# Layer norm slabs of the FFN branch put among those of the attention branch, and a BF16 scratch tensor, in a fused recurrent layer

## The chip, the cores and the metric

The kernel runs on the 8 cores of one Trainium2 chip (two dies of four cores), each with a batch row and a quarter of its query tokens. There is no exchange between cores. The metric is the device time of the slowest core in microseconds, for one launch. Less is better.

## The reference

B = 2, S = 4096, E = 2048, 16 heads of 128, hidden size I = 8192. For all tokens:

```
xn = (x - mean) / sqrt(var + 1e-5)
q, k, v = xn @ W.T + b                 (heads of 128)
s = softmax(causal(q k.T / sqrt(128)) - slope * |i - j|) v @ Wo.T + bo
f = fwht(xn * SU_ug) / 64
h = silu(f @ W_gate.T * sc_g) * (f @ W_up.T * sc_u)
g = silu(fwht(h * SU_dp) / 64 @ W_down.T * sc_d)
out = x + s * g
```

fwht is the normalised Walsh-Hadamard transform.

## The kernel before, in words

Everything is held transposed, features on partitions, tokens along the row. A core needs K and V of all 4096 tokens of its batch row but the rest only for its own 1024 tokens, so it normalises 32 **attention slabs** of 128 tokens (xT, numbers 0 to 31) and 8 **FFN slabs** (xfT, numbers 32 to 39, called FFN slabs 32 to 39). The stages, one after another: (1) normalisation with K and V; (2) Q for its own tokens; (3) attention head by head; (4) the Wo product, stored to the scratch tensor s_scr in HBM; (5) the Hadamard transform of the FFN input; (6) up and gate products; (7) the second transform; (8) the down product with the final combination s * g + x.

Each engine runs its own list of operations in the order in which `OP` recorded them, and waits on the semaphores that an operation names. So the order of calls in the program is the order on every engine.

Stage 1 is built of three functions.

`ln_head(slab)` is the **head**: an x load (L383) on the GpSimd queue (POOL), 512 KB as it lies in SBUF, cast from F32 to BF16, into one of two buffers xTb; it waits until the slab before last has been normalised (ev_xnt). VectorE squares it (sq_scr, L389). TensorE sums x and squares over the features with a column of ones, 16 + 16 matmuls with 1 output row (L395, L400: the statistics). The **row chain** follows: ScalarE copies two rows out of PSUM (L408, L409), VectorE forms the variance (L415, L416), ScalarE the root (L420), VectorE rstd_row and mrstd_row (L424, L425). The rows have one buffer each.

`ln_tail(slab)` is the **tail**: TensorE broadcasts both rows to 128 partitions (L434, L436, F32 matmuls), ScalarE copies them to rstdB and mrstdB, VectorE normalises in 32 chained operations of 128x128 (L448 multiply, L452 subtract), here called the **sweep**. It writes xnT2 (two buffers) for an attention slab, or the slab's place in xnTf, which is kept for stages 2 and 5.

`emit_kv(slab, tail_for)` records the **K and V part**: 16 heads of 16 K matmuls (L469, 128x128), each evicted by ScalarE to kstg, one store of 512 KB to k_scr (L496); then 4 V groups of 16 matmuls (L508, 128x512) in two PSUM banks, each evicted by VectorE to vstg (L521, two buffers) and stored to v_scr from ScalarE's queue (L532). A V group waits until the eviction two groups before it. After the second K head the tail of another slab is recorded.

The loop over slabs is, for i from 0 to 39: head of i; for i = 0 its tail; else K and V of slab i-1 with the tail of i inside, as long as i-1 is an attention slab; from i = 33 on only head and tail. After it the load of Wq (L554), on the GpSimd queue, into the place of Wk, waits for the last V matmul; the Q matmuls (L568) wait for it.

```
    for i in range(NSLAB):
        ln_head(i)
        if i == 0:
            ln_tail(0)
            continue
        kvslab = i - 1
        if kvslab < NSLAB_A:
            emit_kv(kvslab, tail_for=i)
        else:
            ln_tail(i)
```

Stage 4: ScalarE evicts 64 tiles of 128x256 to sstg (L771, F32) and stores them to s_scr (L776). Stage 8: Wd comes in 128 loads of 512 KB into a ring of five (wdring, L980, GpSimd queue); for each of 32 output tiles of 128x512 ScalarE makes g_st (L1014) and issues the loads of ss_st from s_scr (L1021) and of xf_st (L1027); VectorE multiplies g_st by ss_st into o_st (L1033) and adds xf_st (L1037); SyncE stores.

Of the kernel before, what the change touches and what calls it, by code (L numbers as in the profile page):

```python
# [6 lines left out]
F32 = mybir.dt.float32  # L7
# [125 lines left out]
def build_program(cfg):  # L133
# [47 lines left out]
    s_dram = nc.dram_tensor("s_scr", [E, TOKF], F32, kind="Internal").ap()  # L181
# [39 lines left out]
    sstg = [cst(f"sstg{i}", [128, QG], F32) for i in range(2)]  # L221
# [6 lines left out]
    e_stage = 2 * IT * CS * 4 + 2 * FH * 2 + 8 * FH * 4  # L228
# [133 lines left out]
    ev_ld = {}  # L362
    ev_sq = {}
# [11 lines left out]
    def ln_head(slab):  # L375
# [3 lines left out]
        par = slab % 2  # L379
        psem = "xt%d" % par  # L380

# [4 lines left out]
            waits=[ev_xnt.get(slab - 2),  # L386
                   ev_bvB if slab <= 1 else None], dma=psem)
# [3 lines left out]
            waits=[ev_ld[slab], ev_sqmm.get(slab - 1)])  # L391

        def p1_stats(eng, par=par, ev_s=ev_sq[slab]):
# [5 lines left out]
            for ft in range(FT):  # L399
# [5 lines left out]
                           waits=[ev_ld[slab], ev_rows.get(slab - 1)])  # L405

        def p1_rows(eng):
            eng.activation(m_row[:], pb[0][0:1, 0:128], AF.Copy, scale=1.0 / E)  # L408
            return eng.activation(sq_row[:], pb[0][0:1, 128:256], AF.Copy,  # L409
                                  scale=1.0 / E)  # L410
# [17 lines left out]
    def ln_tail(slab):  # L428
# [30 lines left out]
        if slab >= NSLAB_A:  # L459
            ev_cons_all[slab] = ev_sqmm[slab]  # L460
# [681 lines left out]
```

How the kernel before makes its waits and increments, by code:

```python
    def chain(self, eng_name, E, ins):  # L103
        s = self.sem(self.esem[eng_name] + "ch")
        self.cnt[self.esem[eng_name] + "ch"] += 1
        v = self.cnt[self.esem[eng_name] + "ch"]
        ins.then_inc(self.sems[self.esem[eng_name] + "ch"], 1)
        E.wait_ge(self.sems[self.esem[eng_name] + "ch"], v)
# [7 lines left out]
            def body(E, lst=lst):  # L116
                done = {}
                for fn, ws, ev in lst:
                    need = {}
                    for (s, v, _b) in ws:
                        if v > need.get(s, 0):
                            need[s] = v
                    for s, v in need.items():
                        if v > done.get(s, 0):
                            E.wait_ge(self.sems[s], v)
                            done[s] = v
                    ins = fn(E)
                    if ev is not None:
                        ins.then_inc(self.sems[ev[0]], ev[2])
# [263 lines left out]
        def p1_stats(eng, par=par, ev_s=ev_sq[slab]):  # L393
            for ft in range(FT):
                eng.matmul(pb[0][0:1, 0:128], ones128_b[:],
                           xTb[par][:, ft * 128:ft * 128 + 128],
                           start=(ft == 0), stop=(ft == FT - 1))
            eng.wait_ge(sch.sems[ev_s[0]], ev_s[1])
            for ft in range(FT):
                ins = eng.matmul(pb[0][0:1, 128:256], ones128_b[:],
                                 sq_scr[:, ft * 128:ft * 128 + 128],
                                 start=(ft == 0), stop=(ft == FT - 1))
            return ins
```

## Time and profile before

| what | value |
|---|---|
| median of 2 runs | 4624.85 us (4624.21 to 4625.48) |
| the profiled execution | 4626.15 us, span of its slowest core (core 0) 4624.6 us |
| spans of the 8 cores | 4586.8 to 4624.6 us, mean granted TensorE clock 0.864 to 0.868 |
| busy share on core 0 | TensorE 74%, VectorE 40%, ScalarE 21% |
| chain that ended last, by engine | TensorE 64%, VectorE 20%, DMA 6% |

All rows are of core 0. The chain that ended last is followed back from the last instruction, at each step to what released it. In a timeline each row gives the start and the time in us, the engine, the line, the tiles and, in brackets, how long the engine had been idle and who ended that. "PE" is TensorE, "DVE" VectorE, "ACT" ScalarE, "POOL" GpSimd. The granted clock is a share of 2.4 GHz, its lower level 1.2 GHz.

### The profile page before, as it was taken

The numbers are of one execution on the slowest core, as the hardware profiler recorded it, in microseconds if no ns is written. First come the engines' busy times: TensorE is split into PE (matmuls) and PEld (weight loads), VectorE is DVE, ScalarE is ACT, GpSimd is POOL, SyncE is SP. The second block draws the span as 40 slices with busy tenths as digits, with TensorE's granted clock in tenths as the row PEclk, the third lists the DMA queues.
The fourth block names the chain that finished last, engine by engine and source line by source line (L and its number), as shares of the span: only waits on it lengthen the run. The fifth ranks groups of instructions, "written<-read, shape, count | busy, mean of one in ns | idle before, by whom it ended". The sixth has DMA issues, their size and how long they took to land.

```text
span 4624.6 us, 61688 instructions; the slowest of 8 cores (4586.8 to 4624.6 us)
## 1 busy us (share of the span) xinstructions
PE 3428.8 (74%) x22715; PEld 1790.9 (39%) x22715; DVE 1865.3 (40%) x3576; ACT 957.6 (21%) x2347; POOL 294.1 (6%) x309
## 2 busy tenths in 40 slices
PE   0499899999935677888884929999999800725887
PEld 0366666766722222222221804444444300302333
DVE  0244444444452166667773060000000089994001
ACT  0121221211201234444442211111111500000000
POOL 0000000000000000000000001111111100101111
PEclk9999999999957877877776959999999955867999
DMA  9333223232224221111104218888888500736999
GB/s 146 29 47 51 43 43 55 43 53 45 44 31 78 61 55 37 37 37 37 37 19 74 75 13 76 77 77 76 76 78 76 57 0 0 107 48 116 177 174 157
DMA packets 633738, 296.32 MB, mean 64 GB/s; under 512 B 520675, under 2 KB 610787, under 8 KB 631267
## 3 DMA queue, kind: packets, MB, share of 16 engines
q0 software_dynamic: 422880, 191.55, 36.7%
q10 hardware_dynamic: 102912, 58.74, 4.9%
q1 hardware_dynamic: 107652, 42.10, 4.3%
q8 instruction: 187, 3.06, 0.3%
q14 instruction: 107, 0.88, 0.1%
HBM read 433.54 MB, written 50.33 MB: 105 GB/s over the span
## 4 chain that ended last, share of the span: by engine, by line
PE 64%; DVE 20%; DMA 6%; issue 3%; SPq 3%; another core or an unknown queue 2%; ACT 2%; DVEq 0%; ACTq 0%; POOLq 0%
PE pb L856 19%; PE pb L469 9%; PE pb L508 8%; PE pb L695 5%; PE pb L678 5%; PE pb L992 5%; PE pb L674 4%; DMA wdring<-wdT 3%; DVE C L940 3%; DVE C L942 3%; SPq L307 3%; PE pb L568 2%; PE pb L760 2%; DVE rinv L611 2%
## 5 line engine op out<-in xcount | busy, mean ns | idle before, releaser
L856 PE MATMUL pb<-xnTf,wring 128*128 128x512 bf16 x4096 | 886.2, 380 | 1.1 <-ACT xnTf L826 1.1
L992 PE MATMUL pb<-U,wdring 128*128 128x512 bf16 x2048 | 464.1, 389 | 429.9 <-DVE U L952 247.4
L707 DVE SCALAR_TENSOR_TENSOR pb<-mwin_s,slopes_l,pb 128x256 f32<-128x256 f16 x1019 | 484.8, 482 | 434.2 <-PE pb L695 415.5
L856 PEld LDWEIGHTS pb<-xnTf,wring 128*128 128x128 bf16 x4096 | 401.2, 98 | 486.2 <-issue 4.3
L717 ACT ACTIVATE ET<-pb 128x256 bf16<-128x256 f32 x1019 | 390.2, 384 | 485.5 <-DVE pb L707 394.2
L469 PE MATMUL pb<-xnT,wk_b 128*128 128x128 bf16 x8192 | 487.1, 222 | 0.0
L469 PEld LDWEIGHTS pb<-xnT,wk_b 128*128 128x128 bf16 x8192 | 473.0, 100 | 11.2 <-issue 1.1
L992 PEld LDWEIGHTS pb<-U,wdring 128*128 128x128 bf16 x2048 | 202.1, 100 | 691.6 <-issue 468.6
L508 PE MATMUL pb<-wv_b,xnT 128*128 128x512 bf16 x2048 | 447.2, 379 | 0.0
L880 DVE TENSOR_TENSOR U<-A_st,B_st 128x1024 bf16<-128x1024 f32 x64 | 78.4, 1226 | 823.0 <-ACT B_st L872 823.0
L674 PE MATMUL pb<-ET,vh 128*128 128x256 bf16 x1019 | 331.5, 325 | 9.3 <-DMA vh<-v_scr 3.6
L695 PE MATMUL pb<-q_sb,kh 128*128 128x256 bf16 x1019 | 307.1, 323 | 25.6 <-DMA kh<-k_scr 25.6
L678 PE MATMUL pb<-ET,ones_b 128*1 128x256 bf16 x1019 | 311.2, 305 | 0.0
L508 PEld LDWEIGHTS pb<-wv_b,xnT 128*128 128x128 bf16 x2048 | 199.0, 98 | 234.2
L521 DVE TENSOR_TENSOR vstg<-pb,bvB 128x512 bf16<-128x512 f32 x128 | 88.0, 691 | 382.3 <-PE pb L508 245.3
L484 ACT ACTIVATE kstg<-pb,bk_l 128x128 bf16<-128x128 f32 x512 | 188.2, 367 | 242.4 <-PE pb L469 242.4
L448 DVE TENSOR_TENSOR xn_scr<-xTb,rstdB 128x128 f32<-128x128 bf16 x640 | 187.0, 292 | 126.5 <-ACT mrstdB L443 63.0
L1014 ACT ACTIVATE g_st<-pb,dnvec 128x512 bf16<-128x512 f32 x32 | 22.0, 687 | 881.4 <-PE pb L992 560.0
L678 PEld LDWEIGHTS pb<-ET,ones_b 128*1 128x1 bf16 x1019 | 80.5, 79 | 268.0 <-issue 247.7
L618 PE MATMUL pb<-rinv,ones_f 1*128 1x256 f32 x128 | 63.7, 590 | 161.5 <-DVE rinv L611 161.5
L1033 DVE TENSOR_TENSOR o_st<-g_st,ss_st 128x512 f32<-128x512 bf16 x32 | 22.1, 692 | 372.2 <-DMA xf_st<-xfT 201.8
L452 DVE TENSOR_TENSOR xnT<-xn_scr,mrstdB 128x128 bf16<-128x128 f32 x512 | 149.6, 292 | 53.6 <-DVE xn_scr L448 1.0
(85 smaller groups left out, 2530.9 us busy)
## 6 DMA issues: line engine op xcount, KB each, us to landing
wdring<-wdT POOLq DMA_DIRECT2D x128, 512.0 KB, 12.9
wring<-wupT POOLq DMA_DIRECT2D x64, 512.0 KB, 7.8
wring<-wgT POOLq DMA_DIRECT2D x64, 512.0 KB, 7.8
xTb<-xT POOLq DMA_DIRECT2D x32, 512.0 KB, 11.0
k_scr<-kstg ACTq DMA_DIRECT2D x32, 512.0 KB, 5.2
v_scr<-vstg ACTq DMA_DIRECT2D x128, 128.0 KB, 2.1
kh<-k_scr SPq DMA_DIRECT2D x16, 1024.0 KB, 6.5
vh<-v_scr SPq DMA_DIRECT2D x16, 1024.0 KB, 10.6
```

The source lines that it names most:

```text
L448: sch.chain("vector", eng, eng.tensor_mul(xn_scr[:], xTb[par][:, ft * 128:ft * 128 + 128], rstdB[:]))
L452: ins = eng.tensor_sub(dst, xn_scr[:], mrstdB[:])
L469: ins = eng.matmul(bank[:, 0:128], wk_b[:, (ft * H + hch) * 128:(ft * H + hch) * 128 + 128], xnT2[par][:, ft * 128:ft * 128 + 128], start= ...
L484: return eng.activation(kstg[par][:, hch * 128:hch * 128 + 128], bank[:, 0:128], AF.Identity, bias=bk_l[:, hch:hch + 1])
L508: ins = eng.matmul(bank[:, 0:512], xnT2[par][:, ft * 128:ft * 128 + 128], wv_b[:, ft * E + vch * 512:ft * E + vch * 512 + 512], start=(ft ...
L674: eng.matmul(pvb[:, 0:QG], vh[hp][:, rho * 128:rho * 128 + 128], ETs[e4][:], start=(idx == 0), stop=(idx == W - 1))
L678: return eng.matmul(pb[6 + par][0:1, 0:QG], ones128_b[:], ETs[e4][:], start=(idx == 0), stop=(idx == W - 1))
L695: return eng.matmul(pb[b4][:, 0:QG], kh[hp][:, rho * 128:rho * 128 + 128], q_ap, start=True, stop=True)
L707: eng.scalar_tensor_tensor(pb[b4][:, 0:QG], mwin_s[:, coff:coff + QG], slopes_l[:, h:h + 1], pb[b4][:, 0:QG], ALU.mult, ALU.add)),
L717: eng.activation(ETs[e4][:], pb[b4][:, 0:QG], AF.Exp)),
L856: ins = eng.matmul(pb[bk0 + u][:, 0:UCH], wring[slot][:, ft * 128:ft * 128 + 128], xnTf[:, ft * TOKF + u * UCH:ft * TOKF + u * UCH + UCH], ...
L992: ins = eng.matmul(pb[bk0 + e4][:, 0:FHT], wdring[slot][:, iti * 512 + e4 * 128: iti * 512 + e4 * 128 + 128], Uap(it, tk0, FHT), start=(it ...
```

## The change

Stage 1: `ln_head` and `ln_tail` take a second argument, the position `li` in a list `emit_order`; the buffers xTb and xnT2 and the waits on the slab before and before last now go by positions. The rows and rstdB/mrstdB have two halves. The list has two FFN slabs after each eight attention slabs: 0 to 7, 32, 33, 8 to 15, 34, 35, 16 to 23, 36, 37, 24 to 31, 38, 39. `pump(limit)` records heads up to a position and, before the head at position p, any tail at p-2 or earlier. Before K and V of slab ki all heads up to two positions after it are recorded. `emit_kv` calls `tail_cb` after its second K head, which records the waiting tails that are FFN slabs or attention slabs up to ki+1, the first of them first. The first two Q matmul groups wait for the last K evictions.

The scratch tensor s_scr, its staging sstg and the tile ss_st become BF16 instead of F32; the tiles after it move up in SBUF.

```
-    s_dram = nc.dram_tensor("s_scr", [E, TOKF], F32, kind="Internal").ap()
+    s_dram = nc.dram_tensor("s_scr", [E, TOKF], BF16, kind="Internal").ap()
...
-    rstdB = cst("rstdB", [128, 128], F32)
+    rstdB = cst("rstdB", [128, 256], F32)
...
-    sstg = [cst(f"sstg{i}", [128, QG], F32) for i in range(2)]
+    sstg = [cst(f"sstg{i}", [128, QG], BF16) for i in range(2)]
...
-    ss_st = at("ss_st", [128, 2 * FH], F32, p4c + FH * 4)
+    ss_st = at("ss_st", [128, 2 * FH], BF16, p4c + FH * 4)
...
-            waits=[ev_xnt.get(slab - 2),
-                   ev_bvB if slab <= 1 else None], dma=psem)
+            waits=[ev_xnt.get(pprev),
+                   ev_bvB if li <= 1 else None], dma=psem)
...
-            if hch == 1 and tail_for is not None:
-                ln_tail(tail_for)
+            if hch == 1:
+                tail_cb()
...
+    step = NSLAB_A // max(1, NSLAB_F // 2)
+    fi = NSLAB_A
+    for a in range(NSLAB_A):
+        emit_order.append(a)
+        if (a + 1) % step == 0 and fi < NSLAB:
+            emit_order.append(fi)
+            emit_order.append(fi + 1)
+            fi += 2
...
+    def pump(limit):
+        while li[0] < NSLAB and li[0] <= limit:
+            while tailq and tailq[0][1] <= li[0] - 2:
+                pop_tail()
+            s = emit_order[li[0]]
+            ln_head(s, li[0])
+            tailq.append((s, li[0]))
+            li[0] += 1
+
+    pump(1)
+    pop_tail()
+    for ki in range(NSLAB_A):
+        pump(min(NSLAB - 1, pos_attn[ki] + 2))
+
+        def tail_cb(ki=ki):
+            while tailq and (tailq[0][0] >= NSLAB_A
+                             or tailq[0][0] <= ki + 1):
+                pop_tail()
+        emit_kv(ki, pos_attn[ki] % 2, tail_cb)
```

TensorE's list from the V matmuls of slab 7 to K of slab 8, before (the L395/L400 pair is the statistics of a head, L434/L436 the broadcast of a tail, xTb_105 and xTb_106 the two x buffers, xnT_107 and xnT_108 the two normalised ones):

```order
L508 MATMUL pb<-wv_b,xnT_108 128x512 x64
L395 MATMUL pb<-xTb_106,ones_b 1x128 x16
L400 MATMUL pb<-sq_scr,ones_b 1x128 x16
L469 MATMUL pb<-xnT_107,wk_b 128x128 x32
L434 MATMUL pb<-rstd_row,ones_f 128x128
L436 MATMUL pb<-mrstd_row,ones_f 128x128
L469 MATMUL pb<-xnT_107,wk_b 128x128 x224
```

and in the changed kernel, where the same operations are at L400/L405, L449/L451, L491 (K) and L530 (V):

```order
L530 MATMUL pb<-wv_b,xnT_108 128x512 x64
L400 MATMUL pb<-xTb_105,ones_b 1x128 x16
L405 MATMUL pb<-sq_scr,ones_b 1x128 x16
L400 MATMUL pb<-xTb_106,ones_b 1x128 x16
L405 MATMUL pb<-sq_scr,ones_b 1x128 x16
L449 MATMUL pb<-rstd_row,ones_f 128x128
L451 MATMUL pb<-mrstd_row,ones_f 128x128
L400 MATMUL pb<-xTb_105,ones_b 1x128 x16
L405 MATMUL pb<-sq_scr,ones_b 1x128 x16
L491 MATMUL pb<-xnT_107,wk_b 128x128 x32
L449 MATMUL pb<-rstd_row,ones_f 128x128
L451 MATMUL pb<-mrstd_row,ones_f 128x128
```

One head stood before K of slab 8; now three heads and a tail do: heads of slabs 8, 9 and 10, and between the last two the tail of slab 8 itself. The same stands before K of slabs 16 and 24.

TensorE's list at the start, from the first head to the first K matmuls, before:

```order
L395 MATMUL pb<-xTb_105,ones_b 1x128 x16
L400 MATMUL pb<-sq_scr,ones_b 1x128 x16
L434 MATMUL pb<-rstd_row,ones_f 128x128
L436 MATMUL pb<-mrstd_row,ones_f 128x128
L395 MATMUL pb<-xTb_106,ones_b 1x128 x16
L400 MATMUL pb<-sq_scr,ones_b 1x128 x16
L469 MATMUL pb<-xnT_107,wk_b 128x128 x32
```

and in the changed kernel:

```order
L400 MATMUL pb<-xTb_105,ones_b 1x128 x16
L405 MATMUL pb<-sq_scr,ones_b 1x128 x16
L400 MATMUL pb<-xTb_106,ones_b 1x128 x16
L405 MATMUL pb<-sq_scr,ones_b 1x128 x16
L449 MATMUL pb<-rstd_row,ones_f 128x128
L451 MATMUL pb<-mrstd_row,ones_f 128x128
L400 MATMUL pb<-xTb_105,ones_b 1x128 x16
L405 MATMUL pb<-sq_scr,ones_b 1x128 x16
L491 MATMUL pb<-xnT_107,wk_b 128x128 x32
```

Two heads and a tail stood before K of slab 0; now three heads do, with the tail of slab 0 behind the second.

TensorE's list from the head before K of slab 6 to its V matmuls, before:

```order
L395 MATMUL pb<-xTb_106,ones_b 1x128 x16
L400 MATMUL pb<-sq_scr,ones_b 1x128 x16
L469 MATMUL pb<-xnT_107,wk_b 128x128 x32
L434 MATMUL pb<-rstd_row,ones_f 128x128
L436 MATMUL pb<-mrstd_row,ones_f 128x128
L469 MATMUL pb<-xnT_107,wk_b 128x128 x224
```

and in the changed kernel:

```order
L400 MATMUL pb<-xTb_105,ones_b 1x128 x16
L405 MATMUL pb<-sq_scr,ones_b 1x128 x16
L491 MATMUL pb<-xnT_107,wk_b 128x128 x32
L449 MATMUL pb<-rstd_row,ones_f 128x128
L451 MATMUL pb<-mrstd_row,ones_f 128x128
L449 MATMUL pb<-rstd_row,ones_f 128x128
L451 MATMUL pb<-mrstd_row,ones_f 128x128
L491 MATMUL pb<-xnT_107,wk_b 128x128 x224
```

K of slab 6 now carries two tails, that of slab 7 and that of FFN slab 32, and on VectorE their two sweeps stand one behind the other, both ahead of the four V evictions of slab 6. The same holds for slabs 14, 22 and 30. Behind the V matmuls of slab 31 nothing is left on TensorE before Q. On the GpSimd queue the Wq load still follows the last x load.

## Rows read from the trace of the kernel before

**Rows 1.** Chain that ended last, merged: start us, us, what.

```profile
1269.46 13.83 PE pb L508 x64
1304.95 1.88 PE pb L400 x16
1325.85 1.88 PE pb L400 x16
...
1446.94 112.63 PE pb L568 x512
```

**Rows 2.** Windows: us, busy (count) of PE, PEld, DVE, ACT, POOL, PEclk, DMA, GB/s.

```profile
1283.00:1390.00 107.00, 25.19 (x208) 21.23 (x207) 63.13 (x187) 5.83 (x25) 6.27 (x6) 0.53 0.21 21
```

**Rows 3.** DMA issues by line (last column: us to landing), and the GpSimd queue's timeline.

```profile
wk_b<-wkT POOLq DMA_DIRECT2D x1, 8192.0 KB, 60.9
...
wo_b<-woT POOLq DMA_DIRECT2D x1, 8192.0 KB, 53.3
...
1389.44 1.15 POOL L554 DMA_DIRECT2D wq_b<-wqT  x1
```

**Rows 4.** Waits of TensorE, 200 to 1280 us: total us, times, longest.

```profile
PE pb L434 <- DVE mrstd_row L425: 38.6, 30, 1.4
```

**Rows 5.** Timeline of one attention slab, 874 to 908 us.

```profile
873.95 1.05 PE L395 MATMUL pb<-xTb,ones_b 128*1 128x128 bf16 x16
...
874.80 1.22 DVE L389 TENSOR_TENSOR sq_scr<-xTb 128x2048 bf16<-128x2048 bf16 x1
...
876.16 1.05 PE L400 MATMUL pb<-sq_scr,ones_b 128*1 128x128 bf16 x16 [1.16 <-DVE sq_scr L389]
...
877.15 1.96 PE L469 MATMUL pb<-xnT,wk_b 128*128 128x128 bf16 x32
...
880.05 0.28 DVE L425 TENSOR_TENSOR mrstd_row<-m_row,rstd_row 1x128 f32<-1x128 f32 x1
...
881.09 12.78 PE L469 MATMUL pb<-xnT,wk_b 128*128 128x128 bf16 x224
...
881.78 0.29 DVE L448 TENSOR_TENSOR xn_scr<-xTb,rstdB 128x128 f32<-128x128 bf16 x1 [1.45 <-ACT mrstdB L443]
...
893.70 13.98 PE L508 MATMUL pb<-wv_b,xnT 128*128 128x512 bf16 x64
...
894.12 0.29 DVE L452 TENSOR_TENSOR xnT<-xn_scr,mrstdB 128x128 bf16<-128x128 f32 x1
...
895.31 1.14 POOL L383 DMA_DIRECT2D xTb<-xT  x1 [32.94 <-DVE xnT L452]
...
905.10 0.69 DVE L521 TENSOR_TENSOR vstg<-pb,bvB 128x512 bf16<-128x512 f32 x1 [3.46 <-DMA v_scr<-vstg]
```

**Rows 6.** Landing of the x loads (L383, all 40), and in 1340 to 1385 us.

```profile
DMA to landing us min/median/max: 6.8/10.5/14.4
...
xTb<-xfT POOLq DMA_DIRECT2D x2, 512.0 KB, 7.1
```

**Rows 7.** Timeline of the start, 170 to 200 us.

```profile
170.62 0.28 DVE L425 TENSOR_TENSOR mrstd_row<-m_row,rstd_row 1x128 f32<-1x128 f32 x1
...
187.19 1.86 PE L400 MATMUL pb<-sq_scr,ones_b 128*1 128x128 bf16 x16 [13.16 <-DVE sq_scr L389]
...
188.99 3.09 PE L469 MATMUL pb<-xnT,wk_b 128*128 128x128 bf16 x32
...
193.03 7.14 PE L469 MATMUL pb<-xnT,wk_b 128*128 128x128 bf16 x123
```

**Rows 8.** Waits, 4200 to 4624 us.

```profile
PE pb L992 <- DMA wdring<-wdT: 47.2, 23, 5.5
```

**Rows 9.** DMA queues, 4320 to 4600 us: packets, MB, share of 16 engines.

```profile
q10 hardware_dynamic: 4608, 8.39, 12.9%
```

**Rows 10.** Chain that ended last, in the Wo stage.

```profile
2581.43 3.80 DMA s_scr<-sstg
```

**Rows 11.** Groups of instructions by form: second transform's first step on VectorE.

```profile
L920 DVE TENSOR_TENSOR C<-U,U 128x512 f32<-128x512 bf16 x64 | 44.0, 688 | 64.8 <-ACT U L902 61.5
```

More of the change, by code:

```diff
@@ L362, in build_program @@
     ev_ld = {}
+    ev_bcE = {}
     ev_sq = {}
@@ L373, in build_program, with ln_head @@
     ev_vevac = {}
-    def ln_head(slab):
+    emit_order = []
+    def ln_head(slab, li):
         is_ffn = slab >= NSLAB_A
@@ L404, in ln_head, with p1_rows @@
         ev_sqmm[slab] = OP("tensor", p1_stats,
[L405 to L409, printed above, removed]
+                           waits=[ev_ld[slab], ev_rows.get(prev)])
+        pr = lambda t, q=par: t[0:1, q * 128:q * 128 + 128]
+        def p1_rows(eng, par=par):
+            eng.activation(pr(m_row), pb[0][0:1, 0:128], AF.Copy,
+                           scale=1.0 / E)
+            return eng.activation(pr(sq_row), pb[0][0:1, 128:256], AF.Copy,
@@ L418, in ln_head @@
         ev_var = OP("vector", p1_var, waits=[ev_rows[slab]])
-        ev_sd = OP("scalar", (lambda eng: eng.activation(
-            msq_row[:], var_row[:], AF.Sqrt)), waits=[ev_var])
-        def p1_rstd(eng):
-            sch.chain("vector", eng, eng.reciprocal(rstd_row[:], msq_row[:]))
-            return eng.tensor_mul(mrstd_row[:], m_row[:], rstd_row[:])
-        ev_rstd[slab] = OP("vector", p1_rstd, waits=[ev_sd])
-    def ln_tail(slab):
+        ev_sd = OP("scalar", (lambda eng, par=par: eng.activation(
+            pr(msq_row), pr(var_row), AF.Sqrt)), waits=[ev_var])
@@ L429, in ln_tail, with p1_rstd, p1_bc @@
+        def p1_rstd(eng, par=par):
+            sch.chain("vector", eng,
+                      eng.reciprocal(pr(rstd_row), pr(msq_row)))
+            return eng.tensor_mul(pr(mrstd_row), pr(m_row), pr(rstd_row))
+        ev_rstd[slab] = OP("vector", p1_rstd,
+                           waits=[ev_sd, ev_bcE.get(pprev)])
+    def ln_tail(slab, li):
         is_ffn = slab >= NSLAB_A
         cc0 = (slab - NSLAB_A) * 128 if is_ffn else slab * 128
-        par = slab % 2
-        def p1_bc(eng):
-            eng.matmul(pb[1][:, 0:128], ones1_f[:], rstd_row[:], start=True,
+        par = li % 2
+        prev = emit_order[li - 1] if li >= 1 else None
+        pprev = emit_order[li - 2] if li >= 2 else None
+        pr = lambda t, q=par: t[0:1, q * 128:q * 128 + 128]
+        def p1_bc(eng, par=par):
+            eng.matmul(pb[1][:, 0:128], ones1_f[:], pr(rstd_row), start=True,
@@ L435, in p1_bc @@
                        stop=True)
[L436 removed]
+            return eng.matmul(pb[1][:, 128:256], ones1_f[:], pr(mrstd_row),
                               start=True, stop=True)
         ev_bc = OP("tensor", p1_bc,
[L439 to L444 removed]
+                   waits=[ev_rstd[slab], ev_bcast_ev.get(prev), ev_ones])
@@ L446, in p1_xnt, with p1_bcev @@
+        ev_bcE[slab] = ev_bc
+        def p1_bcev(eng, par=par):
+            eng.copy(rstdB[:, par * 128:par * 128 + 128], pb[1][:, 0:128])
+            return eng.copy(mrstdB[:, par * 128:par * 128 + 128],
+                            pb[1][:, 128:256])
+        ev_bcast_ev[slab] = OP("scalar", p1_bcev,
+                               waits=[ev_bc, ev_xnt.get(pprev)])
         def p1_xnt(eng, par=par, is_ffn=is_ffn, cc0=cc0):
```

98 lines of the change are left out of this document (52 added, 46 removed).

## The prediction

> **What bounds the kernel now.** I read the page's chain shares and its slices first: TensorE carries most of the chain, but the kernel is a row of stages with different limits, so I went to the stage that the diff touches, 153 to 1447 us, and read its chain of waits. Up to 1283.3 us (1269.46 + 13.83) the K and V matmuls of 32 attention slabs follow one another. Then the statistics of the FFN slabs stand 20.9 us apart (1304.95, 1325.85) and the Q matmuls start only at 1446.9 [rows 1]. The view by windows says what that is: in 1283 to 1390 us TensorE works 25 of 107 us at a granted clock of 0.53 and VectorE 63 us: a serial chain of VectorE and tiny matmuls [rows 2]. Last comes Wq: its load is issued at 1389.44, behind the last x load on the GpSimd queue, and Q, which waits for it, starts 57.5 us after that, so it takes 57.4 [rows 1, 3]. So behind the last V matmul lie 163.6 us (1446.94 - 1283.3), of which the load is 57.4.
>
> Inside the attention part a slab takes 33.7 us, almost all of it K and V matmuls; the one wait that the change touches is that of the broadcast matmul (L434) for mrstd_row: 38.6 us over 30 slabs, 1.3 us each [rows 4].
>
> **Clocks of one slab**, counted from the end of the V matmuls before it (874.0) [rows 5]: squares end at 2.1, the second statistics start at 2.2, 32 K matmuls run 3.2 to 5.1, mrstd_row is done at 6.4 (3.1 us after the statistics end), the other 224 K matmuls start at 7.1. The sweep of 32 normalising operations runs 7.8 to 20.4, that is 12.7 us, the next x load is issued at 21.3, 0.9 us after it, and V ends at 33.7. I use these for every step below.
>
> **1. The end of the stage.** The FFN slabs 38 and 39 now normalise while slabs 30 and 31 are in K and V, and no x load stands behind the last V matmul. Wq still cannot start earlier, since it overwrites Wk. So the gap becomes 0.5 (queue) + 57.4 + 0.1 = 58.0 us instead of 163.6: **-105.6 us**. What is late next is the Wq load itself, bare. The loads of Wo and Wk, of the same size, took 53.3 and 60.9 us [rows 3], so the term lies between -109.7 and -102.1.
>
> **2. The wait for mrstd_row.** The tail that now stands after two K groups belongs to a slab whose head stood one slab earlier, so its row is long ready. That holds for slabs 0 to 5, 8 to 13, 16 to 21 and 24 to 29; in the other eight the FFN tail still follows its own head directly. Slab 0 is counted in step 5, so 23 x 1.3 = **-29.9 us**.
> What hid the x load before is gone, however. Head s+2 now stands before K of slab s, and its load can only be issued when the sweep of slab s has freed the buffer. The sweep starts at 6.7 instead of 7.8 (rstd of the new head at 6.4, then the broadcast), ends at 19.3, and the load goes out at 20.2. The statistics need it at 32.4, and a delay up to 0.8 us more is covered by the squares, which wait for the last V eviction anyway. So a landing of up to 13.0 us is free. The rows give 10.5 in the median and 14.4 at most [rows 6]; at 14.4 the slab gets back to its old length. From none late to all late this is 0 to +29.9; I take the side of the median, **+2**.
>
> **3. Slabs 6, 14, 22, 30: two sweeps in one slab.** VectorE now does slab 7 and then FFN slab 32: 6.7 + 12.7 + 12.7 = 32.1. The V evictions stand behind both. TensorE fills two banks (V from 20.1), then waits for the first eviction, 32.8 instead of 23.5; two more V groups of 3.5 us follow, and V ends at 39.8, 6.1 late. The third eviction can wait for the first store, as the one at 905.10 does for 3.46 us [rows 5]; here the matmuls before it hide most of that, and I add 0.7 of between 0 and 3.5: 6.8 each. 4 x 6.8 = **+27** (24 to 38).
>
> **4. Slabs 8, 16, 24: a drain.** Here three heads stand before K. Head 12 (position in the new list) needs the buffer of attention slab 8, which is swept only now. From the end of V: mrstd 6.4; squares of head 11 7.7; its statistics and row chain 4.3, 12.0; the sweep of slab 8 24.7; the queue 25.6; the load, alone on the DMA engines as in the FFN stretch, 7.1 [rows 6], 32.7; squares 33.9; statistics at the low clock, 35.9. K starts there instead of at 3.2, and its first 32 matmuls take 3.09 instead of 1.96, as they did after the idle time at the start [rows 5, 7]: 33.8 us each. Nothing covers it, since the only work ready on TensorE stands behind the statistics in its queue. 3 x 33.8 = **+101.5** (to 112 at the 10.5 us landing). This step gives back what step 1 brings.
> The Trainium skill ("DMA: Bandwidth & Descriptors", Anatomy of one DMA) fits such a load as about 2.0 us plus its bytes over 436 GB/s, an estimate of 3.2 us for 512 KB; the quietest rows here say 7.1, so this case's trace does not agree. By the rule the drains and the start would be some 18 us cheaper together; I go by the trace.
>
> **5. The start.** Head 1 and head 2 now stand before K of slab 0, and load 2 waits for the sweep of slab 0. mrstd of slab 0 170.9, squares 172.2, statistics 174.2, row chain 177.3, sweep 190.0, issue 190.9. The landing lies between 7.1 and 10.5 [rows 6]; I take 9, as no K or V store runs yet but all cores load together: 199.9. Squares, statistics, 32 cold K matmuls and the broadcast: 207.3, against 193.03 now [rows 7]. **+14.3** (12.4 to 15.8).
>
> **6. s_scr in BF16.** Stores in the Wo stage halve; the chain runs through one of them, for 3.8 us [rows 10], so the gain is 0 to 3.8, and I take 0.5, as a single wait of 64 stores shows. The loads of ss_st halve in the down projection, where TensorE waits 47.2 us in all for wdring and the ScalarE queue takes 12.9% of the DMA time of 280 us, half of it ss_st by bytes [rows 8, 9]. Half of ss_st is 9 us there, 13 over the 398 us of the stretch; between none of it and all of it I take **-7**, as TensorE waits only in bursts. Both together **-7.5** (0 to -17).
> The Trainium skill ("VectorE: DVE Perf Modes", Rules for kernel authors) promises tensor_tensor twice the rate on dense BF16, and the product in the combination now reads two BF16 tiles. It writes F32, though: a row with just these types took 688 ns for 512 columns [rows 11], no faster than today's product, so this trace gives nothing; by the rule the last four products would save about 1.2 us.
>
> **Sum.** -105.6 - 29.9 + 2 + 27 + 101.5 + 14.3 - 7.5 = +1.8 us. The profiled execution took 4626.15 us (span 4624.6), 1.3 above the median of the runs. So 4628.0 profiled, 4627 as a median.
>
> **Rivals.**
> A. The drains do not happen or are mostly hidden, so that the FFN work is really folded away: the sum without step 4 is -99.7, 4525 us. For it speaks only that this is how 5 of 6 boundaries work; against it the two x buffers and the order of TensorE's queue.
> B. The x load becomes the limit in every slab. It decides above a landing of 14.4 us: the slab is then 20.2 + landing - 0.8 long. At 17 us that is 36.4 against 33.7, 28 boundaries, +74, and the -27.9 of step 2 are gone: 1.8 + 27.9 + 74 = +104, 4729 us. For it: the K and V stores share the DMA engines with the load at just that time, in all eight cores. Against it: no landing of 40 above 14.4, and the same transfers meet at the same points as before.
> C. Start, double sweeps, drains, late loads and the Wq load are all at their upper bounds and s_scr brings nothing: 15.8 + 0 + 38 + 112 - 102.1 = +64, 4688 us. It is still inside 2%.
>
> **Chances.** The forecast with its bounds, and C with it: 0.88 (C with what lies near it 0.12). A 0.04, B 0.08. So faster by over 2% (under 4532) 0.04, within 2% 0.88, slower by over 2% (over 4717) 0.08; 2% is about what a measurement of this kernel can tell from no change. With all terms at their better bounds the sum is 12.4 - 29.9 + 24 + 101.5 - 109.7 - 17 = -19, 4606 us; I go 17 us (half of one drain) further towards A, to 4589. Upwards I go to C: 4688.
>
> **What would show it.** Right: Q starts 58 us after the last V matmul, at about 1456 us; three holes of some 34 us in front of K of slabs 8, 16 and 24, ended by an x load and its squares; the wait of the broadcast matmul falls from some 30 cases to some 8; slabs 6, 14, 22 and 30 are 6 to 7 us longer; K of slab 0 is in full swing at 207. Wrong: TensorE waiting for xTb at most boundaries (B), no holes (A), a wait for wdring that is still 47 us, or any change in the attention and up/gate stages, which the change does not touch.

## The result, and the profile after

The changed kernel takes 4602.16 us (median of 29 runs), the kernel before 4626.24 us (26 runs). The ratio is 0.994, with a 95% interval of 0.9921 to 0.9959: some 28 us faster, between 19 and 37. This is inside 2% and inside the stated range, but the forecast was +2 us, and the interval excludes that. Some runs of most kernels are disturbed on one die and several per cent longer; the ratios and intervals leave them out (the medians don't), and where a profile below is of such a run (the squares moved, the third buffer), only cores 0 to 3, on the other die, are read.

First the page of the changed kernel: its span and TensorE's share.

```profile
span 4590.7 us, 61740 instructions; the slowest of 8 cores (4568.0 to 4590.7 us)
...
PE 3420.6 (75%) x22715; PEld 1781.7 (39%) x22715; DVE 1864.2 (41%) x3576; ACT 956.3 (21%) x2347; POOL 294.1 (6%) x309
```

Core 0 is the slowest core in both profiles, and its span fell by 33.9 us (4624.6 to 4590.7). Stage 1 as a whole, read by where Q starts, gave 15.0 of that (1446.94 to 1431.94); all the rest, 18.9, comes behind Q. In the mean over the 8 cores the span fell by 25.3 us, 9.0 of it up to Q and 16.3 behind it.

**The end of the stage.** The chain that ended last, merged, as in [rows 1]: start us, us, what.

```profile
1351.95 12.71 PE pb L491 x224
1364.66 13.81 PE pb L530 x64
1378.48 53.22 another core or an unknown queue
...
1431.94 112.80 PE pb L621 x512
```

The last V matmul and Q are now 53.5 us apart instead of 163.6. The 53.22 us piece is the Wq load, which the chain doesn't name; the waits of TensorE do. Here they are for 150 to 1500 us (total us, times, longest), to be read beside [rows 4]:

```profile
PE pb L400 <- DMA xTb<-xT: 100.2, 5, 23.0
PE pb L621 <- DMA wq_b<-wqT: 53.5, 1, 53.5
PE pb L405 <- DVE sq_scr L394: 47.4, 35, 3.0
PE pb L530 <- DVE vstg L543: 17.2, 4, 4.4
PE pb L449 <- DVE mrstd_row L436: 8.8, 8, 1.4
```

The wait of the broadcast matmul (L449, L434 before) has gone from 30 cases to 8. In its place stand four new waits for an x load (at the start and in the three drains; the fifth case of the first line, for the very first slab, is in the kernel before too) and four for a V eviction (fourth line).

**A drain**, before K of slab 8: timeline (start us, us, engine, line, tiles; in brackets the idle time and who ended it).

```profile
467.17 1.05 PE L400 MATMUL pb<-xTb,ones_b 128*1 128x128 bf16 x16
...
474.84 1.87 PE L405 MATMUL pb<-sq_scr,ones_b 128*1 128x128 bf16 x16 [2.68 <-DVE sq_scr L394]
...
492.83 1.14 POOL L388 DMA_DIRECT2D xTb<-xT  x1 [36.82 <-DVE xnT L471]
...
500.24 1.86 PE L400 MATMUL pb<-xTb,ones_b 128*1 128x128 bf16 x16 [22.39 <-DMA xTb<-xT]
...
503.75 2.27 PE L491 MATMUL pb<-xnT,wk_b 128*128 128x128 bf16 x32
```

V of slab 7 ends at 467.2. The third head's load can go out only at 492.83, when the sweep of slab 8 has freed its buffer, and TensorE stands idle for it for 22.39 us. K starts at 503.75, 36.6 us after V.

**A slab with two sweeps**, slab 6:

```profile
397.81 0.45 PE L449 MATMUL pb<-rstd_row,ones_f 1*128 1x128 f32 x2 [0.84 <-DVE mrstd_row L436]
...
398.42 14.31 PE L491 MATMUL pb<-xnT,wk_b 128*128 128x128 bf16 x224
...
422.95 1.28 DVE L543 TENSOR_TENSOR vstg<-pb,bvB 128x512 bf16<-128x512 f32 x2
...
423.78 9.80 PE L530 MATMUL pb<-wv_b,xnT 128*128 128x512 bf16 x32 [4.14 <-DVE vstg L543]
...
433.51 1.05 PE L400 MATMUL pb<-xTb,ones_b 128*1 128x128 bf16 x16
```

The second half of the V matmuls waits 4.14 us for VectorE, which evicts only behind both sweeps. Note also that the 224 K matmuls take 14.31 us here.

**A plain slab**, slab 11, to be laid beside [rows 5]:

```profile
599.83 1.05 PE L405 MATMUL pb<-sq_scr,ones_b 128*1 128x128 bf16 x16 [1.16 <-DVE sq_scr L394]
...
600.82 1.96 PE L491 MATMUL pb<-xnT,wk_b 128*128 128x128 bf16 x32
...
602.71 0.48 PE L449 MATMUL pb<-rstd_row,ones_f 1*128 1x128 f32 x2
...
603.35 12.78 PE L491 MATMUL pb<-xnT,wk_b 128*128 128x128 bf16 x224
...
629.87 1.05 PE L400 MATMUL pb<-xTb,ones_b 128*1 128x128 bf16 x16
```

The broadcast matmul has no bracket any more: it follows the 32 K matmuls at once.

**All slabs at once.** A single slab hides what follows, so I took the start of each slab's K part from the timeline of core 0 (a period is the time from one K start to the next), and the time from its first to its last K matmul. These are worked out from the timeline, us:

| | before | changed |
|---|---|---|
| first K matmul of slab 0 | 188.99 | 199.95 |
| K start to K start, plain slabs (23 of them changed) | 33.7 in the clean ones | 32.3 (742.8 for 23) |
| slabs 6, 14, 22, 30 | 33.7 to 35.2 | 42.3, 42.7, 41.1, 42.7 (168.9) |
| slabs 7, 15, 23 (with the drain behind them) | 33.7 or 33.8 | 67.0, 67.0, 69.2 (203.2) |
| all 31 periods | 1063.6, that is 31 x 33.7 and 18.9 more | 1148.0 |
| K part: 15.3 to 15.9 | none | 24 slabs |
| K part: 16.7 to 17.0 | 26 slabs | 3 slabs (7, 15, 31) |
| K part: 18.2 to 18.4 | 6 slabs (core 4: 9) | 5 slabs (6, 14, 22, 23, 30) |
| last K start to Q | 194.4 | 84.0 |

The 18.9 us are what I had missed. The kernel before doesn't run 33.7 us per slab: six periods are 1.5 longer because the K part is (9.4 us together), and five more lie between 34.2 and 37.0 (9.3 together). The first kind is on every core: 6 to 9 long K parts, 9.4 to 13.9 us. The second is not: it makes 9.5 us on core 0 and 6.0 on core 1, and at most 0.7 on each of the other six. In the mean over the cores the kernel before is 14.7 us over 31 x 33.7. For the K parts the view by windows of the kernel before has the reason (columns as in [rows 2]); these are slab 12, with a long K part, and slab 13, with a short one:

```profile
606.80:621.20 14.40, 14.40 (x226) 14.20 (x226) 9.35 (x32) 5.49 (x16) 0.70 (x1) 0.88 0.00 1
642.00:656.00 14.00, 14.00 (x232) 13.12 (x231) 9.36 (x32) 5.86 (x17) 0.12 (x1) 1.00 0.01 3
```

TensorE is busy throughout both, and in the first its granted clock is 0.88 instead of 1.00: for a part of the K matmuls it was at the 1.2 GHz level. Ahead of it lie two waits of 1.16 and 1.37 us with 3 us of matmuls between them; but slab 13 has the same two (1.16 and 1.44 us) and keeps 1.00. The Trainium skill ("TensorE: Matmul & The Clock Gate", Part 1) calls the low level the default that activity releases, and ties its return to idleness; in this trace it returns with no more idle time than that, and not each time. In the changed kernel the plain slab is clean, and the slab with two sweeps isn't:

```profile
398.40:412.70 14.30, 14.30 (x226) 14.25 (x226) 10.48 (x36) 5.49 (x16) 1.14 (x1) 0.88 0.02 3
...
603.00:616.00 13.00, 13.00 (x229) 12.80 (x228) 9.67 (x33) 5.48 (x16) 0.00 (x0) 1.00 0.01 1
```

The longest of the other periods (slab 9, 37.0) shows in the timeline of the kernel before as a V store that landed late, with the evictions, the squares and TensorE behind it; slabs 10 and 4, the next longest, have the same with waits of 7.3 and 5.4 us (the last row, the sums of squares, takes 1.86 us instead of the 1.05 of [rows 5]: the clock is low here as well):

```profile
528.39 1.29 DVE L521 TENSOR_TENSOR vstg<-pb,bvB 128x512 bf16<-128x512 f32 x2 [8.10 <-DMA v_scr<-vstg]
...
530.95 1.86 PE L400 MATMUL pb<-sq_scr,ones_b 128*1 128x128 bf16 x16 [3.65 <-DVE sq_scr L389]
```

In the changed kernel no eviction on core 0 waits longer than 3.9 us for a V store. On the other cores the longest wait is 4.3 to 7.8 us before and 3.4 to 4.8 after.

**The rest of the kernel.** Mean over the 8 cores, us: from Q to the first down matmul 2511.0 before, 2508.4 after; first to last down matmul 631.7 and 620.2; behind it 22.5 and 20.3. Core 0, the slowest, gained more in the down product: 646.2 to 629.0. In both profiles the cores fall into four with a long down product (633.6 to 646.2 before, 626.3 to 629.0 after) and four with a short one (621.9 to 625.6, and 610.4 to 615.4). They aren't the same four: cores 4 and 7 are among the short ones before and the long ones after. Core 0's waits for Wd, against [rows 8], and the queue q10 (it carries the loads of ss_st and xf_st) at 4320 to 4560 us, in the changed kernel and then in the kernel before:

```profile
PE pb L1048 <- DMA wdring<-wdT: 33.0, 20, 3.5
...
q10 hardware_dynamic: 4608, 6.29, 10.8%
...
q10 hardware_dynamic: 4320, 7.87, 14.1%
```

### The profile page after: what moved, and what is told of

The parts are those of the page before. It is cut to its first block, busy times and chain, and to the rows that moved or that the text cites. A ratio compares the mean times of both kernels' runs of the same rounds, so it can differ in the third digit from the quotient of the medians.

```text
span 4590.7 us, 61740 instructions; the slowest of 8 cores (4568.0 to 4590.7 us)
## 1 busy us (share of the span) xinstructions
PE 3420.6 (75%) x22715; PEld 1781.7 (39%) x22715; DVE 1864.2 (41%) x3576; ACT 956.3 (21%) x2347; POOL 294.1 (6%) x309
## 4 chain that ended last, share of the span: by engine, by line
PE 65%; DVE 20%; DMA 5%; issue 3%; SPq 3%; another core or an unknown queue 2%; ACT 1%; DVEq 0%; ACTq 0%; POOLq 0%
PE pb L912 19%; PE pb L530 9%; PE pb L491 9%; PE pb L751 5%; PE pb L734 5%; PE pb L1048 5%; PE pb L730 4%; DVE C L996 3%; DVE C L998 3%; DMA wdring<-wdT 3%; SPq L307 3%; PE pb L816 2%; PE pb L621 2%; DVE rinv L667 2%
## 5 line engine op out<-in xcount | busy, mean ns | idle before, releaser
L491 PE MATMUL pb<-xnT,wk_b 128*128 128x128 bf16 x8192 | 481.0, 221 | 0.0
L491 PEld LDWEIGHTS pb<-xnT,wk_b 128*128 128x128 bf16 x8192 | 467.3, 99 | 10.8 <-issue 1.0
L530 PE MATMUL pb<-wv_b,xnT 128*128 128x512 bf16 x2048 | 457.7, 385 | 17.2 <-DVE vstg L543 17.2
L530 PEld LDWEIGHTS pb<-wv_b,xnT 128*128 128x128 bf16 x2048 | 201.0, 99 | 259.7 <-issue 32.1
L751 PEld LDWEIGHTS pb<-q_sb,kh 128*128 128x128 bf16 x1019 | 95.9, 99 | 193.4 <-issue 130.5
```

Source lines behind the costliest of these rows:

```text
L491: ins = eng.matmul(bank[:, 0:128], wk_b[:, (ft * H + hch) * 128:(ft * H + hch) * 128 + 128], xnT2[par2][:, ft * 128:ft * 128 + 128], start ...
L530: ins = eng.matmul(bank[:, 0:512], xnT2[par2][:, ft * 128:ft * 128 + 128], wv_b[:, ft * E + vch * 512:ft * E + vch * 512 + 512], start=(ft ...
L751: return eng.matmul(pb[b4][:, 0:QG], kh[hp][:, rho * 128:rho * 128 + 128], q_ap, start=True, stop=True)
```

## The experiments

Two questions were open: what of the 28 us is the scratch tensor and what the order, and why the order didn't cost the 9 us that steps 1 to 5 gave. The first four kernels ran together on one chip, with the kernel before.

### The scratch tensor alone

The kernel before, with s_scr, sstg and ss_st in BF16 as in the change, and nothing else.

```
-    s_dram = nc.dram_tensor("s_scr", [E, TOKF], F32, kind="Internal").ap()
+    s_dram = nc.dram_tensor("s_scr", [E, TOKF], BF16, kind="Internal").ap()
```

> The kernel before with s_scr, sstg and ss_st in BF16 and nothing else. Theory (the scratch is worth more than the 7.5 us forecast, because ss_st loads and Wd loads compete for the DMA engines all through the down product): from the first to the last down matmul 620 us instead of 632 in the mean of the 8 cores, the tail after it 20 instead of 22.5, stage 1 unchanged (K to the last V 1090 us, 163 us from there to Q); in all 12 to 18 us faster, about 4610. Rival (the down product got faster in the changed kernel because its cores reach it at other times, not because of the BF16 loads): down product 632 us as before, total 4620 to 4627.

Measured: 4603.18 us, ratio 0.9951 (0.9934 to 0.9969), about -23 us. Stage 1 is as before (K start to last V 1090.8 in the mean against 1089.9), and so is Q to down (2509.8). The down product takes 622.7 instead of 631.7, the tail 20.1 instead of 22.5: -11.4 in the mean over cores. That is the theory's picture; only the total moved by more than its 12 to 18 us. One reason is that the slow cores gain more: in the runs behind the ratio the four slower cores of a run go from 4616.2 to 4597.5 us in the mean (-18.7) and the four quicker ones from 4591.5 to 4581.0 (-10.5). The product of g_st and ss_st itself takes 692 ns on core 0 in both kernels. The waits for Wd on core 0:

```profile
PE pb L992 <- DMA wdring<-wdT: 25.7, 25, 2.8
```

So most of the 28 us can be had from the scratch tensor, through the down product of the cores that were slowest. The new order adds some 5 us, with overlapping intervals.

### The new code with the old order

The changed kernel, whose list is now 0 to 39.

```
-        if (a + 1) % step == 0 and fi < NSLAB:
+        if False:
```

> The changed kernel with the list in natural order, 0 to 39: the head two slabs ahead and the tail without its wait stay, no pair of FFN slabs stands between attention slabs. Theory (each normal slab takes 32.3 us, a pair in between costs 34 + 8.5 us, about what two FFN slabs cost at the end, 2 x 20.9): no drains, K starts at 198, last V at about 198 + 32 x 32.3 + 9 = 1241 us, then six serial FFN slabs of 20.9 us of which the last two stand beside the Wq load, Q at about 1380 instead of 1432; total about 4545. Rival (the interleaving itself is what pays): Q at 1440 or later, total at or above the changed kernel's 4592 to 4598.

Measured: 4569.9 us, ratio 0.9881 (0.9863 to 0.9899). This is 0.6% less than the changed kernel: **putting the FFN slabs among the others costs more than it brings.** K start to last V is 1041.3 us in the mean (1177.9 changed, 1089.9 before). Where I was wrong is the end: last V to Q is 163.3 us, not shorter, so Q starts at 1401.9 instead of 1380. The x load, which the FFN slabs of the kernel before mostly hide, is bare now for the last four of them: on the chain of core 0 these loads start at 1265.35, 1292.40, 1318.99 and 1345.97, some 27 us apart where the slabs of [rows 1] stood 20.9 apart. The last one, still one serial piece behind another (the 40.85 us are the rest of the Wq load):

```profile
1345.97 6.32 DMA xTb<-xfT
1352.52 1.87 PE pb L400 x16
...
1360.56 40.85 another core or an unknown queue
1401.92 13.17 PE pb L621 x49
```

What the new code gains, it gains in the attention slabs, where a head now stands one slab ahead of its tail: all periods of core 0 up to slab 29 but the first are 32.2 to 32.4 us.

### The wait put back

The changed kernel, whose broadcast matmul also waits for the row chain of the newest head, though it doesn't need it.

```
-                   waits=[ev_rstd[slab], ev_bcast_ev.get(prev), ev_ones])
+                   waits=[ev_rstd[slab], ev_rstd[emit_order[len(ev_rstd) - 1]], ev_bcast_ev.get(prev), ev_ones])
```

> The changed kernel in which every broadcast matmul waits, besides its own row, for the row of the newest head: the wait for mrstd_row is back in 24 slabs, the head two slabs ahead and the list stay. Theory (the removed wait is worth 1.4 us itself and some 0.6 more per slab by drops of TensorE's clock to the low level in the K matmuls and by late squares): slabs of 33.7 us with some K runs of 14.2 us among those of 12.7 and a granted clock of 0.88 in them; K to the last V 1178 + 24 x 2 = 1226, total +45 to +50, about 4642. Rival (the rest of the gain comes from x loads and V stores that collide less, x landing 8.7 us in place of 10.5): only 1.4 per slab, no 14.2 us K runs, 1178 + 34 = 1212, total about +34, 4630.

Measured: 4647.43 us, ratio 1.0052 (1.0033 to 1.0071). K start to last V went up by 54.3 us in the mean: nearer to the 48 of the theory than to the rival's 34, and above both. The waits of TensorE at 210 to 1200 us on core 0, and its chain:

```profile
PE pb L449 <- DVE mrstd_row L436: 43.8, 28, 3.3
```

```profile
620.93 14.24 PE pb L491 x224
...
656.11 12.71 PE pb L491 x224
```

The bare wait is back (43.8 us in 28 cases), and with it the K run of 14.24 us beside the one of 12.71. The granted clock in these two K runs is 0.88 and 1.00. Worked out slab by slab on core 0 (+51.4 in all): 19 of the 24 plain slabs are longer by 1.2 to 1.8 us, the other five by 2.9; together 41.5. The three drains add 6.1 and the four double sweeps 3.8. **So the wait costs its 1.4 us, and in every fifth slab twice that**, through the clock that drops behind it. No core of this run has slabs lengthened by late V stores as core 0 of the kernel before has them, but the longest waits for one are 3.8 to 6.2 us; whether the broadcast's wait bears on them isn't settled by this.

### The tail after the fourth K head, in the kernel before

One number: the tail of the next slab is recorded after four K heads instead of two, so that the row chain has 64 matmuls of cover.

```
-            if hch == 1 and tail_for is not None:
+            if hch == 3 and tail_for is not None:
```

> The kernel before, with the tail recorded after the fourth K head instead of the second: only the wait for mrstd_row goes, the look-ahead, the list and the scratch are those of before. Theory (wait plus clock): 32 slabs of about 32.3 us, no K run of 14.2 us, K to the last V about 1090 - 32 x 1.9 = 1030, total about 4565. Rival (1.4 us per slab only, and the collisions stay, since the x load is issued at the same point of a slab): 1090 - 45 = 1045, x landing still 10.5 in the median, total about 4580.

Measured: 4583.74 us, ratio 0.9904 (0.9879 to 0.993). K start to last V falls to 1042.4 us in the mean, 47.5 less; the size is the rival's (1045), not the theory's (1030), but the rest of the rival fails: it had the x loads still landing after 10.5 us, and on core 0 it is 7.4 in the median. A clean slab goes only from 33.7 to 32.6, since a small wait for ScalarE's eviction takes part of the 1.4 us back: that makes 35 us of 32 slabs, and the rest is the time over 33.7 (14.7 in the mean, 18.9 on core 0), nearly all of it. Waits of core 0 at 210 to 1200 us, and the window of 220 to 1220:

```profile
PE pb L400 <- DVE sq_scr L389: 36.3, 31, 1.5
PE pb L469 <- ACT kstg L484: 6.2, 32, 0.3
```

```profile
220.00:1220.00 1000.00, 955.61 (x10862) 698.95 (x10921) 461.45 (x1264) 210.13 (x645) 35.44 (x31) 1.00 0.30 50
```

The same window of the kernel before:

```profile
220.00:1220.00 1000.00, 922.44 (x10371) 678.91 (x10369) 437.19 (x1193) 199.13 (x611) 33.16 (x29) 0.98 0.31 47
```

The granted clock is 1.00 over 1000 us, no K part takes over 16.3 us, and every period is between 32.6 and 33.3. The longest wait for the squares is 1.5 us instead of 3.6. No slab of core 0 is late by a V store any more (longest wait 3.7 us; on core 2 it is 5.6), though nothing was changed about the stores. All this from one number, without a third head or a list.

### No ss_st loads

The kernel before without the load of ss_st; the product takes xf_st in its place, so the attention result is left out of the output.

```
-                ev_ss = OP("scalar", (lambda eng, eo=eo, tk0=tk0, par=par:
...
+                ev_ss = None
```

> The kernel before without the 32 loads of ss_st: the product in the combination multiplies g_st by xf_st instead, so the output leaves the attention result out; all else is as before. Theory (each byte of ss_st costs the down product the same): first to last down matmul 632 us with 256 KB loads, 623 with 128 KB (BF16 scratch), so about 613 with none, and the total some 35 to 45 us under the kernel before, about 4585. Rival (what the BF16 scratch gave was the smaller piece at bursts and the last bytes cost nothing): 620 to 623 and a total of about 4603, as with the BF16 scratch.

Measured: 4585.44 us, ratio 0.9895 (0.9788 to 1.0003), an interval that includes no change; and in its profile a down product of 601.0 us in the mean, where the theory had 613. The loads do cost the down product its time, so the rival is out. How the two halves of the bytes share it can't be read closely. With 256 KB per tile the down product is 631.7 us in the kernel before and 631.0 in the run with the tail after the fourth head; with 128 KB it is 622.7 with the scratch tensor alone, but 619.6 to 620.2 in the changed kernel and the two runs made from it, and 613.9 and 615.9 in two runs below (both small edits; the third buffer again). So half the bytes are worth 9 to 18 us and the other half 13 to 22, and a straight line isn't excluded. The two steps also aren't alike: halving the bytes leaves the number of loads and of their packets as it was, taking the loads away takes these with it. No run separates bytes from packets.

### Both small edits

The scratch tensor in BF16 and the tail after the fourth K head, in the kernel before.

> The kernel before with the tail after the fourth K head and the scratch in BF16, no interleaving and no look-ahead. Theory (the two gains add, and the interleaving of the changed kernel earns nothing beyond them): K to the last V 1042 us, 163 from there to Q, down product 623; -45 from the wait and -23 from the scratch, total about 4560, faster than the changed kernel by 35 us. Rival (they share the same time): total at or above 4575.

Measured: 4545.31 us, ratio 0.9812 (0.9706 to 0.9917). K start to last V 1042.3, down 613.9: the two gains add up (the total is even 15 us below the theory's 4560), and the result is some 50 to 60 us below the changed kernel.

### Is it the wait for the squares or the number of waits?

The kernel before, with the sums of squares recorded after the second K head and the tail after the fourth: then nothing waits ahead of K.

```
             if hch == 1 and tail_for is not None:
+                ln_head2(tail_for)
+            if hch == 3 and tail_for is not None:
                 ln_tail(tail_for)
```

> The kernel before with the second half of the statistics (the sums of squares) recorded after the second K head and the tail after the fourth: the wait for the squares (1.2 us per slab) goes, and the wait for mrstd_row stays at about 1.3 us. Theory (two idle stretches within 5 us at each slab boundary bring the clock down, one alone does not): no time at the low clock in 227 to 1200 us against 37 us before, slab 32.4 us, K to the last V about 1090 - 32 x 1.7 = 1036. Rival (the wait for mrstd_row by itself brings the clock down): low clock about as before, K runs of about 1.5 us above the others in a third of the slabs, K to the last V 1090 - 32 x 1.2 = 1052.

Measured: a ratio (0.9892, 0.9735 to 1.005) that decides nothing, so I read core 0 of the profile. Waits at 210 to 1200 us, two slabs of the timeline, and the window:

```profile
PE pb L475 <- ACT kstg L492: 32.7, 30, 1.2
```

```profile
626.04 1.05 PE L475 MATMUL pb<-xnT,wk_b 128*128 128x128 bf16 x16 [1.16 <-ACT kstg L492]
...
627.83 12.52 PE L475 MATMUL pb<-xnT,wk_b 128*128 128x128 bf16 x192
...
660.11 1.05 PE L475 MATMUL pb<-xnT,wk_b 128*128 128x128 bf16 x16 [1.08 <-ACT kstg L492]
...
661.89 10.99 PE L475 MATMUL pb<-xnT,wk_b 128*128 128x128 bf16 x192
```

```profile
220.00:1200.00 980.00, 944.58 (x10333) 697.63 (x10332) 435.57 (x1190) 194.66 (x609) 33.11 (x29) 0.96 0.31 48
```

The experiment did not isolate what it was made for: the row chain now stands in ScalarE's queue between two K evictions, and TensorE waits 1.1 us for the second. But it says something else. With this one wait per slab, inside the K part, there is more low clock than before (0.96 against 0.98): 26 of the 32 K parts of core 0 (20 on each of cores 1 to 3) take 19.3 us or more and six take 17.8 to 18.0. Of the two slabs shown the first has a granted clock of 0.91 in 626 to 646 us, the second 1.00 in 660 to 680. My theory that two waits close together are needed is refuted. K start to last V is 1081 us on core 0 and 1072 on the other three, above the 1036 of the theory and the 1052 of the rival. What separates a wait that drops the clock from one that doesn't stays open.

### A third x buffer

Built on the kernel with both small edits. The FFN slabs get an x buffer and a pair of broadcast tiles of their own, and FFN slab 32 + j runs through attention slab 4j + 1: its load one slab ahead, squares behind the sweep of the next attention slab, statistics and broadcast between V groups, its sweep in pieces between V evictions of this slab and the next. Every attention slab keeps its buffer and its order.

```
+        buf = xTf if is_ffn else xTb[slab % 2]
...
+            if fs is not None and vch == 0:
+                ln_stats(fs)
+            if fs is not None and vch == 1:
+                ln_sweep(fs, 0, 4)
+            if fs is not None and vch == 2:
+                ln_sweep(fs, 4, 7)
+                pend.extend([(slab, fs, (0, 7, 11)), (slab, fs, (1, 11, 15)),
+                             (slab, fs, (2, 15, 16))])
```

> The FFN slabs folded in without a drain: from the tail-after-4 kernel with BF16 scratch, a third x buffer for FFN slabs, one FFN slab in every fourth attention slab, its statistics and broadcast between the V groups and its sweep cut in five pieces between the V evictions of that slab and the next. Theory (the drains and double sweeps were what the interleaving cost, and the FFN slabs themselves need only 3.5 us of TensorE each): K to the last V 1042 + 8 x 4 = 1074 us, 54 from there to Q, Q at about 1315 instead of 1432, total about 4450 to 4475. Rival (VectorE, with a sweep of 12.7 us more in eight slabs, holds V evictions and squares back): K to the last V above 1110, total 4500 or more.

No ratio can be given for this run. In its profile, cores 0 to 3 have 1059.2 us from K start to last V and 53.1 from there to Q. The same kernel ran again for the time:

> The same kernel as in the run with the third buffer, which had too few undisturbed executions for a ratio. Its undisturbed cores spanned 4427 to 4453 us, so both theories of that run are past; expected here: total 4455 to 4462 us, a ratio of 0.963 to 0.966 to the kernel before.

Measured: 4459.95 us, ratio 0.9627 (0.9551 to 0.9702): **faster than both kernels**, by 3.7% against before. The chain of the slowest core, and its window:

```profile
1251.88 52.99 another core or an unknown queue
1305.11 95.07 PE pb L622 x429
```

```profile
250.00:1240.00 990.00, 949.91 (x10878) 694.00 (x10877) 528.85 (x1483) 212.60 (x662) 38.81 (x34) 1.00 0.32 51
```

The end of the stage is near what step 1 priced (53 us from V to Q against 58), no drain stands against it, and the clock is 1.00. Periods of core 0 are 32.6 to 32.8 (the first 33.3, the last, with no head behind it, 29.5) and, with an FFN slab in them, 35.3 to 35.6: an FFN slab folded in costs 2.8 us, 22 in all, where the list of the change pays 136 (the 102.1 of the drains and the 34.1 of the double sweeps).

## Why the prediction was right or wrong

The sum for core 0 up to Q, from the table of all slabs, each term against the clean slab of 33.7 us that the prediction used:

| step | forecast | measured | how |
|---|---|---|---|
| 5, start | +14.3 | +10.4 | 199.95 - 188.99, and slab 0 itself 33.1 - 33.7 |
| 2, wait and late loads | -27.9 | -32.3 | 742.8 - 23 x 33.7 |
| 3, double sweeps | +27 | +34.1 | 168.9 - 4 x 33.7 |
| 4, drains | +101.5 | +102.1 | 203.2 - 3 x 33.7 |
| 1, end | -105.6 | -110.4 | 84.0 - 194.4 |
| before's slabs over 33.7 | 0 | -18.9 | 31 x 33.7 - 1063.6 |
| sum up to Q | +9.3 | -15.0 | 1431.9 - 1446.9 |
| 6, behind Q | -7.5 | -18.9 | 4590.7 - 1431.9 against 4624.6 - 1446.9 |
| whole | +1.8 | -33.9 | |

**Right.** The mechanisms of steps 1, 3, 4 and 5. A drain was to push K out by 33.8 us and took 34.0 in the mean (102.1 over three): TensorE's order and two buffers do set it, so rival A falls. The load in it took 7.16 us where I put 7.1; the estimate of 3.2 us from the Trainium skill ("DMA: Bandwidth & Descriptors", Anatomy of one DMA) would have made each drain 4 us shorter, and no row bears that out. Step 1 was 4.8 short, since Wq landed in 52.7 us where I kept 57.4; my lower bound, from the load of Wo, was the better row. Rival B falls too (by its own terms it was +76, not +74: 28 x 2.7): no plain slab waits for x, whose landing on core 0 is even shorter than in [rows 6]:

```profile
DMA to landing us min/median/max: 6.6/8.7/11.1
```

Q was to start at 1456 and starts at 1431.94.

**Step 5** was 4 us too dear. I put the landing of the third load at 9 us and it took 6.88, and the first 32 K matmuls took 2.27 where I carried 3.09 over from [rows 7]. Their granted clock is 0.84 (199.9 to 202.2 us) and was 0.61 there (189.0 to 192.1): now the two statistics blocks, 3.5 us of matmuls, stand directly ahead of them, then it was one. In the timeline of the changed kernel:

```profile
196.45 1.86 PE L400 MATMUL pb<-xTb,ones_b 128*1 128x128 bf16 x16 [22.22 <-DMA xTb<-xT]
...
199.95 2.27 PE L491 MATMUL pb<-xnT,wk_b 128*128 128x128 bf16 x32
```

**Step 3** was 7 us too cheap: 8.5 for a slab instead of 6.8. The order of events is as worked out (the eviction of 0.69 us behind both sweeps), but the broadcast matmul's wait in these four slabs, which I left as it was, has the low clock and 1.5 us behind it (14.31 in the row above).

**Step 2 failed, and it is the main error.** Its two rows were right: the wait is 1.3 us, and a plain slab is 1.4 shorter than a clean slab of before. But what I took for the slab of before was one good slab, [rows 5]; eleven of 31 weren't. Six pay 1.5 us more for a clock drop in the K part (9.4), and five are long for the most part through late V stores (9.3). I priced the wait by its idle time and gave the rest of the unevenness no term at all. Over all cores the clock is the larger part: 9.4 to 13.9 us on each, while the V stores cost 9.5 and 6.0 us on two cores and at most 0.7 on six. In the changed kernel both are gone from the plain slabs: no K part over 15.9 us in the 24 slabs whose broadcast doesn't wait, and five of 18.3 or 18.4 among the eight in which it does. That the clock drop comes with the wait was shown by putting it back, and once more by covering the wait in the kernel before (clock 1.00, -47.5 us). For the V stores this is not shown. With the order of before, such slabs make 10.8 and 6.8 us on cores 2 and 3 in the run with the scratch tensor alone, and at most 0.8 on any core in the run without the ss_st loads, whose stage 1 is the same; with the other orders no core has more than 3. So core 0 may have lost its 9.3 us by chance as well as by the change, and what makes the stores late was not found. The mean period (1063.6 / 31 = 34.3) beside the slab of 33.7 would have shown me 19 us that no term explained.

**Step 6 failed by size.** -7.5 with a floor of -17; measured alone -11.4 in the mean over cores, and about -23 in the time that counts. I priced q10's share on core 0 and took a little over half of it, as if all cores gained alike. But the metric is the slowest core, and its down product stood 14 us above the mean (646.2 against 631.7). The four slower cores of a run lie 25 us behind the four quicker ones before and 16 with the scratch tensor alone, and they aren't always the same four; by that tensor the slower four gain 18.7 us and the others 10.5. The store half of the step, 0.5 us, is too small to be seen.

**What the change does in the end.** The list of FFN slabs moves 110 us of exposed work away from the end of the stage and pays 136 for it in drains and double sweeps. The head one slab ahead costs some 10 us at the start, with the list or without it (K of slab 0 starts at 187.0 us in the mean before, 198.6 in the changed kernel, 199.1 with the old order). That the kernel is faster all the same comes from this head, which takes the wait out of the attention slabs, and from the scratch tensor: the same code with the old order is 0.6% faster still.

## What to carry to other kernels

Before pricing a wait, compare the mean period of the loop with the slab that you read row by row; what lies between them belongs to somebody, here on all cores a clock that dropped behind a wait of 1.4 us, and on two of them also stores that landed late. Look at more than one core before calling such a part a property of the kernel. When work is moved into the shadow of other work, count the buffers: with two, three heads ahead of K cannot be fed, and the shadow turns into a drain; a third buffer and pieces placed between evictions made the same idea pay. Where the slowest core counts, price a shared resource on that core and on the spread, not on the mean.

## What was unexpected in the hardware

- With one wait of 1.1 us for a K eviction, between two groups of 128x128 matmuls, 26 of 32 K parts of core 0 (20 on cores 1 to 3) were 1.5 us longer than the others, and the mean granted clock over 980 us was 0.96. With waits of at most 0.3 us in the K part and 1.2 for the squares ahead of it, it was 1.00 over 1000 us. The three slabs 7, 15 and 31 of core 0 of the changed kernel have the broadcast's wait and no drop (16.7 to 16.9), and so have most of the 26 short slabs of the kernel before, so a wait doesn't always bring one.
- On core 0 VectorE's longest wait for a V store is 8.1 us in the kernel before and at most 3.9 with the other orders (the change, its wait put back, FFN slabs last, tail after four heads), and x loads land after 10.5 us in the median before and 7.4 to 9.2 in these. The other cores show less of a difference: 4.3 to 7.8 us before, and up to 6.2 with the wait put back. What sets these landings, and how much of it is chance, was not tried.
- The loads of ss_st are some 4 of the 41.8 MB that core 0 moves at 4320 to 4560 us in the kernel before, and yet the down product follows them: 631.7 and 631.0 us with 256 KB a tile, 613.9 to 622.7 with 128 KB, 601.0 with none. Within the one profile of the kernel before it differs by 24 us from core to core (621.9 to 646.2).
